# A three-layer transformer on one core: where softmax and query norms are divided out, and when weights are prepared

## What is computed

```
x = x + 0.5 * ffn(layernorm(x))          # two layers of local attention
x = x + attention(layernorm(x))          # 16 heads of 8, causal, softmax over 256 keys
x = x + 0.5 * ffn(layernorm(x))          # the same two layers

layer:     q, k, v = split(shift(x) @ wqkv)              # 8 heads of 64
           q, k = l2norm(q) * qs, l2norm(k) * ks         # per token and head
           q, k = rotary(q, k)
           x = x + local_attention(8 * q, k, v) @ wo     # windows of 64, look back one window
           x = x + (a * gelu(g)) @ w2 + b2               # a, g = layernorm(shift(x)) @ w1 + b1
attention: softmax(q k' / sqrt(8) + causal) @ v @ Wo + bo
```

## Time and profile before

| | before |
|---|---|
| median of 3 runs | 1858.02 us |
| lowest, highest | 1854.99, 1860.14 us |
| the profiled execution | 1866.13 us |
| its span, first to last instruction | 1864.3 us |
| mean granted clock of TensorE, of its full speed | 0.972 |

### The profile page before, as it was taken

The page is one execution under the profiler, slowest core; times in us unless marked ns, Lnnn a source line. Parts: engine busy times, 40 slices in busy tenths (PEclk is TensorE's granted clock), DMA queues, the critical chain, the costliest instruction groups (busy, mean ns, idle before and its releaser), DMA issues.

```text
span 1864.3 us, 51559 instructions
## 1 busy us (share of the span) xinstructions
PE 1680.3 (90%) x18560; PEld 1367.5 (73%) x18560; DVE 1479.3 (79%) x2938; ACT 1564.8 (84%) x4956; POOL 1286.7 (69%) x1528
## 2 busy tenths in 40 slices
PE   2798899989999999998988899899999999989987
PEld 2577778778877777777777677777687777777776
DVE  5788888688788687888889788876778775788886
ACT  1588799888999898998788888799999887988886
POOL 4899974487394657759998999920559570589991
PEclk9799999999999999999999999999999997999999
DMA  4101000000010000010100011000000000001000
GB/s 113 35 10 24 13 10 11 10 18 19 2 27 11 10 20 14 19 31 18 38 25 24 19 24 28 10 2 2 18 11 19 10 18 1 19 19 28 20 16 15
DMA packets 31701, 36.48 MB, mean 20 GB/s; under 512 B 7986, under 2 KB 18652, under 8 KB 31452
## 3 DMA queue, kind: packets, MB, share of 16 engines
q1 hardware_dynamic: 31452, 33.19, 7.4%
HBM read 5.91 MB, written 2.10 MB: 4 GB/s over the span
## 4 chain that ended last, share of the span: by engine, by line
POOL 37%; PE 23%; DVE 15%; ACT 15%; issue 9%; SPq 1%; DMA 0%; POOLq 0%; ACTq 0%; DVEq 0%
POOL rnorm L1031 13%; POOL parts L1021 11%; POOL parts L1035 8%; ACT probs L1090 8%; PE bank L1427 6%; PE bank L1510 4%; DVE parts L1358 4%; PE bank L1586 3%; POOL sums_floor L1028 3%; ACT turned L1108 2%; POOL rstd L1009 2%; DVE neg_max L1264 2%; PE bank L1546 2%; DVE sums L1365 2%; PE bank L1627 1%
## 5 line engine op out<-in xcount | busy, mean ns | idle before, releaser
L1090 ACT ACTIVATE probs<-bank,neg_max 128x128 f32<-128x128 f32 (+1 forms) x1536 | 584.7, 446 | 36.5 <-DVE neg_max L1264 35.5
L1021 POOL TENSOR_TENSOR parts<-parts 128x256 f32<-128x256 f32 x512 | 377.4, 763 | 161.8 <-DVE parts L1358 160.9
L1031 POOL TENSOR_TENSOR rnorm<-sums_floor,neg_half 128x8 f32<-128x8 f32 x256 | 431.9, 1687 | 21.3
L1090 ACT ACTIVATION_READ_ACCUMULATOR probs<-bank,neg_max 128x1 f32 x1536 | 401.5, 268 | 0.0
L1358 DVE TENSOR_TENSOR parts<-bank,rope 128x1024 f32<-128x1024 f32 x256 | 308.8, 1215 | 51.0 <-ACT squares L1137 49.7
L1264 DVE TENSOR_REDUCE neg_max<-bank 128x4 f32<-128x512 f32 (+1 forms) x448 | 287.5, 681 | 73.5 <-PE bank L1479 39.8
L1035 POOL TENSOR_TENSOR parts<-parts,rnorm 128x512 f32<-128x512 f32 x256 | 278.7, 1089 | 37.6 <-POOL rnorm L1031 1.3
L1510 PE MATMUL bank<-ident,probs 128*128 128x128 f32 x1792 | 253.5, 283 | 39.9 <-DVE probs L1279 19.4
L1108 ACT ACTIVATE turned<-bank 128x512 f32<-128x512 f32 x448 | 258.3, 661 | 34.1 <-PE bank L1510 33.5
L1510 PEld LDWEIGHTS bank<-ident,probs 128*128 128x128 f32 x1792 | 205.4, 145 | 78.3 <-issue 33.3
L1007 POOL TENSOR_SCALAR var_eps<-mean_var 128x2 f32<-128x2 f32 x112 | 32.3, 289 | 318.6 <-DVE mean_var L1297 313.6
(11 more groups left out here) (119 smaller groups left out, 3873.4 us busy)
## 6 DMA issues: line engine op xcount, KB each, us to landing
between<-val SPq DMA_DIRECT2D x192, 128.0 KB, 2.3
x_sb<-in_L_attn_x_dram SPq DMA_DIRECT2D x16, 128.0 KB, 2.7
out_dram<-x_sb SPq DMA_DIRECT2D x16, 128.0 KB, 1.9
raw_qkv<-in_L_ffn_wqkv_dram SPq DMA_DIRECT2D x2, 768.0 KB, 5.5
raw_w<-in_L_ffn_w_dram SPq DMA_DIRECT2D x2, 341.0 KB, 4.3
wo<-in_L_ffn_wo_dram SPq DMA_DIRECT2D x2, 256.0 KB
rope<-in_rope_dram SPq DMA_DIRECT2D x1, 256.0 KB, 3.0
w<-in_L_ffn_w_dram SPq DMA_DIRECT2D x2, 128.0 KB
```

The lines of the kernel that those rows point to most:

```text
L1021: last = nc.gpsimd.tensor_tensor(joined[:, :, dst], joined[:, :, dst], sines[:, :, src], ALU.add)
L1031: nc.gpsimd.tensor_tensor(rnorm[:, u], sums_floor[:, u], neg_half[:], ALU.pow).then_inc(sems["pool_step"], 1)
L1090: last = nc.scalar.activation(probs[:, u, block:block + wide].rearrange("p b j -> p (b j)"), bank[:, at:at + P * wide], ACT.Exp, bias=neg_ ...
```

## The change

- **Queries.** `rope_scale` of a q step ends with the power, which goes to a new buffer `q_norm`; the product over 512 columns stays for k only. `row_max` in local attention multiplies the 128x4 maxima by those inverse norms, and `exp_scores` takes them as a per-row scale.
- **Full attention.** The values get a ninth column of ones (`valf`), so that the product gives the row sum too. The turned probabilities (128x128) are now the stationary operand and nine columns of values move: 12 products a unit. The accumulators of the exponentials, the 64 reciprocals on their sums, the spreading products and ACT's copy of them go. DVE takes the reciprocal of the ninth columns in PSUM and scales 128x64 elements. The result has tokens in rows, so a new step **OT** turns it, two blocks a sequence, with a copy on ACT; WOF is one product in place of four; VALF moves 128 weight columns in place of 512, and its copy is as narrow.
- **Preparing.** The third, padded set of `wf` becomes an unpadded `wv`. `COME` holds times for READY 15 and 18, which it did not, and for LNX. The transfers of `bv` and `Wo` come ahead of the bias pieces, of which there are 24 in place of 32 transfers.
- **The order.** `passes` has new durations, and `START_AT`, `STRETCH`, `DUE`, `PHASE_DUE` and `LATER` (now 176 entries) new numbers, so all four orders differ.

```diff
 COME = {
-("READY", 12, 0): 19.0, ("READY", 21, 0): 37.0, ("FOLD", 2, 0): 37.0, ...
+("LNX", 0, 0): 8.5, ("READY", 12, 0): 19.5, ("READY", 15, 0): 19.5, ("READY", 18, 0): 19.5, ("READY", 20, 0): 35.0,
+("FOLD", 2, 0): 35.0, ...
 def passes(step):
     if kind == "X":
-        return [(DVE, 0.61), (ACTE, 0.92 if is_full(ph) and n % 3 else 1.4)]
+        return [(DVE, 0.61 if is_full(ph) else 0.83), (ACTE, (0.74 if n % 3 else 1.06) if is_full(ph) else 1.4)]
     if kind == "V":
-        return [(PE, 1.08), (ACTE, 0.28), (DVE, 0.34)] if is_full(ph) else [(PE, 0.97), (ACTE, 0.5)]
+        return [(PE, 1.5), (DVE, 0.4)] if is_full(ph) else [(PE, 0.97), (ACTE, 0.5)]
-LATER = {}
+LATER = {(0, 0): 75.49, (0, 1): -11.95, ...
 # rope_scale, POOL
+                if step[3] % 2 == 0:
+                    pool.wait_ge(sems["pool_step"], count("pool_step", step))
+                    if left_by(step) is not None:
+                        pool.wait_ge(sems["bank_filled"], count("bank_filled", left_by(step)))
+                    nc.gpsimd.tensor_tensor(q_norm[set_of(step)][:, step[3] // 2], sums_floor[:, u], neg_half[:],
+                                            ALU.pow).then_inc(sems["rope_ready"], 1)
+                    return
 # exp_scores, ACT
-                    last = nc.scalar.activation(probs[...], bank[:, at:at + P * wide], ACT.Exp, bias=neg_max[:, u, row:row + 1],
-                                                accum_out=prob_sum[:, u, row:row + 1])
+                    if is_full(ph):
+                        last = nc.scalar.activation(dst, bank[:, at:at + P * wide], ACT.Exp, bias=neg_max[:, u, row:row + 1])
+                    else:
+                        t, h = row % 2, UNIT * (k // 2) + row // 2
+                        last = nc.scalar.activation(dst, bank[:, at:at + P * wide], ACT.Exp, bias=neg_max[:, u, row:row + 1],
+                                                    scale=q_norm[set_of(step)][:, t, h:h + 1],
+                                                    accum_out=prob_sum[:, u, row:row + 1])
 # row_max, DVE, local attention
+                nc.vector.tensor_reduce(dst, src, AX, ALU.max, negate=True).then_inc(sems["vector_step"], 1)
+                dve.wait_ge(sems["vector_step"], count("vector_step", step))
+                nc.vector.tensor_tensor(dst, dst, norms, ALU.mult).then_inc(sems["max_ready"], 1)
 # values, PE, full attention
-                    for t in range(TILES):
-                        for h in range(UNIT):
-                            nc.tensor.matmul(bank[at:at + PAD_D, T + P * t:T + P * (t + 1)],
-                                             prob_inv[:, i, row:row + 1].to_broadcast([P, PAD_D]), ident[:], ...
-                    for t in range(TILES):
-                        for h in range(UNIT):
-                            last = nc.tensor.matmul(bank[at:at + PAD_D, P * t:T], val[a][:, t, PAD_D * (UNIT * m + h):...],
-                                                    turned[:, u, of:of + T - P * t], ...
+                    for h in range(UNIT):
+                        for n, (t, keys) in enumerate(((0, 0), (1, 0), (1, 1))):
+                            at, of = (FULL_D + 1) * (UNIT * t + h), P * (3 * h + n)
+                            last = nc.tensor.matmul(bank[:, at:at + FULL_D + 1], turned[:, u, of:of + P],
+                                                    valf[a][:, keys, UNIT * m + h], start=(keys == 0), stop=(keys == t),
+                                                    skip_group_check=True)
 # scale_heads, DVE
-                nc.vector.tensor_tensor(o_full[set_of(step)][:, m], bank[:, 0:T], inverse[:], ALU.mult)
+                nc.vector.reciprocal(inv, heads[:, :, :, FULL_D:FULL_D + 1]).then_inc(sems["vector_step"], 1)
+                dve.wait_ge(sems["vector_step"], count("vector_step", step))
+                nc.vector.tensor_tensor(o_full[...][:, :, cols]..., heads[:, :, :, 0:FULL_D], inv.to_broadcast(...), ALU.mult)
 # dense, PE
-                    for c in range(CHUNKS):
-                        last = nc.tensor.matmul(bank[:, 0:T], w[:, c], o[:, c], start=(c == 0), stop=(c == CHUNKS - 1))
+                if kind == "OT":
+                    for t in range(TILES):
+                        last = nc.tensor.transpose(bank[:, P * t:P * (t + 1)], o_full[set_of(step)][:, t], ident[:])
+                if kind == "WOF":
+                    last = nc.tensor.matmul(bank[:, 0:T], wof[:], y_t[s], start=True, stop=True)
-                    last = split_matmul(bank[:], hi[:, tok], lo[:, tok], wf_hi[:, 2], wf_lo[:, 2], True)
+                    last = split_matmul(bank[:, 0:C], hi[:, tok], lo[:, tok], wv_hi[:, 0], wv_lo[:, 0], True)
```

More of the change, by code:

```diff
@@ L109, in dense_parts @@
     return front, back
-DENSE = {"FOLD", "WO", "LNH", "LNT", "W1", "W2", "WOF", "XADD", "STATE", "Q", "VAL", "R", "QF", "VALF"}
+DENSE = {"FOLD", "OT", "WO", "LNH", "LNT", "W1", "W2", "WOF", "XADD", "STATE", "Q", "VAL", "R", "QF", "VALF"}
 POOLED = DENSE | {"T", "V"}
@@ L165 @@
+COME = {("LNX", 0, 0): 8.5, ("READY", 0, 0): 10.0, ("READY", 2, 0): 9.0, ("READY", 6, 0): 19.5, ("READY", 12, 0): 19.5, ("READY", 15, 0): 19.5, ("READY", 18, 0): 19.5,
+        ("READY", 20, 0): 35.0, ("FOLD", 0, 0): 14.0, ("FOLD", 1, 0): 14.0, ("FOLD", 2, 0): 35.0, ("FOLD", 0, 1): 23.0}
 BEGIN = (1.5, 2.0, 1.0, 5.3)
@@ L286, in weights_of @@
         return [("FOLD", 0, 0, DENSE_LAYER[PHASES[ph][1]])]
-    if kind in ("QF", "VALF") and part == 0:
-        m = n // 2 if kind == "QF" else 2
-        return made(("wf_hi", m), ("wf_lo", m))
+    if kind == "QF" and part == 0:
+        return made(("wf_hi", n // 2), ("wf_lo", n // 2))
+    if kind == "VALF" and part == 0:
+        return made(("wv_hi", 0), ("wv_lo", 0))
     if kind == "QF" and part == 1:
-        return made(("biases", 0))
+        return made(("biases", 0), ("table", LAYERS - 1))
     if kind == "WOF":
@@ L361, in needs @@
                     wait(x, 1, x, 0)
-                    wait(unit, 0, x)
+                    if not is_full(ph):
+                        wait(unit, 0, x)
                 for x in turned_for(unit):
@@ L466, in takes @@
             if before is not None:
-                for z in [(y, 1) for y in exps_of(before)] if part == 0 else [(y, 0) for y in turned_for(before)] + [(before, 0)]:
+                for z in [(y, 1) for y in exps_of(before)] if part == 0 else [(y, 0) for y in turned_for(before)]:
                     if z not in done:
@@ L683, in emits @@
         "W2": [{}, {"state_ready": 1}],
+        "OT": [{}, {"heads_turned": 1}],
         "WOF": [{}, {"state_ready": 1}],
```

232 lines of the change are left out of this document (116 added, 116 removed), and 44 rows, old and new, of tables (DUE, LATER).

## The result

The changed kernel takes **2080.22 us** (median of 4 runs, 2072.03 to 2081.93) against 1857.83 (4 runs, 1854.99 to 1860.14): a ratio of 1.119, 95% interval 1.116 to 1.122. It is slower by 222 us, where 24 were forecast. The direction was right; the time lies far outside the range (1813 to 1922).

The account below looks back on a forecast made before the run. PE was taken to bound the kernel, except where queries and keys are made, which POOL paces. The span of 1864.3 + 68 (PE) - 29 (POOL) - 15 (start), converted, gave 1882 us; range 1813 to 1922.

Parts of the forecast that it names:

- I take 0.11: Full attention on PE: each of V's 24 full-load records takes 0.11 us, as PE runs near full clock; +91 us.
- slow rival: Orders stall on wrong durations, or the clock falls under thin products: 1913 us; stalling cases (1900 to 1945) had 0.20.
- bound of +229 us for V alone: Full attention on PE: upper bound if all V records stood 0.2 us apart, 4.8 us a unit.
- three signs of being wrong: 128-column loads closer than 0.11 us, PE's share passing 95%, or the start keeping its 30 us.
- The loads of V: Full attention on PE: 24 full loads make V 2.64 us a unit, +91 us of busy time, covered by nothing.
- ACT's second operand: Local attention: a per-row scale on 1024 exponentials, 0 to +102 us on ACT, upper end taken, not a bound.
- DVE's product: Local attention: 256 products on the maxima, each behind a wait, at most +61 us on DVE.
- POOL's relief: Queries and keys: 128 products fewer, -139 us of POOL's busy time, worth -29 us, the middle of -39 and -19.
- The queries' part: Query normalisation moved from POOL into local attention: -29 us from POOL, with no span added for ACT or DVE.
- The start: First sequence: the scheduler can put weight padding behind its normalisation, so PE begins earlier; -15 us (bounds 0 and -18).
- The order: New orders of all four engines: nothing added, called the widest unknown, with its ends left to rivals.
- The relief of ACT in full attention: 512 accumulator reads (48 us) and 64 copies (23 us) go from ACT; none counted, beside a longer PE.

Follow-up runs that it names:

- b_ones: The kernel before with earlier start and full-attention row sums made on PE by columns of ones, without exponential accumulators or ACT's copy: 1907.72 us, ratio 1.022.

## Why the prediction was wrong, step by step

**Where it failed: "PE runs near full clock in both kinds of stretch", so "I take 0.11".** The clock was read from the kernel before and kept for a kernel whose products had changed. The two prices of a thin record stood there (0.11 and 0.2) as if the clock came from outside and a V merely met it. The runs show that the V brings it about: the same 24 loads with 128 columns keep 0.978, with nine 0.907. It costs 130 us in the orders of before. In the changed kernel the low level lasts 422 - 104 = 318 us longer, by the same 0.44 an estimated 140 us, near the 137 that PE's busy time has over the sum. Of the 318, 54 columns in place of nine take back 196, and 93 to 98 us with them. The other 122 aren't parted: orders alone added 74 and 91 us of low level to the instructions of before. The slow rival named a falling clock in one sentence and let it end at 1913; it needed a price of its own. The bound of +229 us for V alone was in the text and did not enter the range. It read L1580's row as one "at the low level of the clock", which no row shows: the profile has 1.00 from 14.00 to 16.60 us, where those twelve records run. That V does take 0.21 a record at the low level (4.98 / 24) bears the number out, not the reading. None of the three signs of being wrong was about the clock, and none of them came.

**The loads of V: right on PE, too dear at the end.** A V at full clock lasts 2.59 us (2.64 forecast). The forecast for V alone was +91 us of PE's busy time, 96 of span at PE's share of 94.7%; the +68 of the sum is net of the narrower WOF and VALF. With 128 moving columns PE's busy time grew by 78 us and the end came 66 later. So "nothing covers it" is not quite so: PE's idle time gave back some 12 us.

**ACT's second operand: size right, place wrong.** It was taken at 0.1 us each (measured 0.09) and then counted at none, since ACT is "not a bound" at 86%. Alone it cost 53 us in the orders of before. DVE's product was counted only as a brake on POOL's gain, and cost 27. A share of the span says how much an engine works, not whether its work lies in a chain: maximum, exponential, reciprocal, turn and V follow on each other, and every engine's fixed order hands a delay on.

**POOL's relief: mis-sized.** -29 forecast, the middle of -39 and -19; -48 measured alone. Even the end of it without a cap by DVE was too small.

**The queries' part in all:** forecast -29; measured +48 in the orders of before, +30 where either kernel has orders searched for it, and -30 in the changed kernel's own orders. The forecast was a gain only because ACT and DVE stood at nothing in it.

**The start: right in mechanism, somewhat large.** -15 forecast, -9 measured, with the first turn before 17 us as said.

**The order: counted at 0.** It isn't small. The due times of before would have cost the changed kernel some 63 us more; those of the change cost the kernel before some 127. But that orders on wrong durations stall is not where most of the loss came from: with V at its full-clock length the kernel takes as long.

**The relief of ACT in full attention: none counted, and not measured.** ACT waits 76 us more for turned probabilities than before, which fits. But no run takes the accumulators away and changes nothing else: b_ones loads DVE at the same time.

Adding up what was measured in the orders of before: +66 (loads) + 130 (clock) + 48 (queries) - 9 (start) = 235 us, against 222. That this comes so near is partly luck. The changed kernel runs other orders, in which the queries' part measured -30 and not +48, and the narrower WOF and VALF, ACT's relief and what the new orders cost by themselves were never parted.

The Trainium skill, page "TensorE: Matmul & The Clock Gate", section "HAM oscillation — how this bites in real kernels", tells of a clock that falls when PE stands idle waiting for transfers. This trace differs: PE is 94.8 to 98.5% busy in the stretches at 0.71 to 0.80. What is thin here is what a busy PE streams, not its share of the time.

## What to carry to other kernels

A product with a full stationary operand and a few moving columns cost twice here: its loads, and the clock of all that runs around it, though it took only about a quarter of a busy PE's time. Price such a product at the low level of the clock too, and give that case a chance of its own; moving more columns than are needed brought most of the clock back. And an instruction on an engine that isn't the bound is free only if it isn't in a chain between engines that run in fixed orders: here 0.09 us on each of 1024 exponentials, on an engine at 84%, cost more than half of itself at the end. Orders made for one program are no fair test of another: one edit cost 48 us in some orders and gained 30 to 36 in others.

## What the runs showed of the hardware that was not expected

- More work made a kernel faster: 128 moving columns in place of nine, with all else the same, took 130 us off (2059.90 to 1930.31), with a granted clock of 0.978 in place of 0.907.
- PE's clock stood at its lower level with the engine 98% busy (0.74 in 350 to 450 us of that kernel).
- DVE's reciprocal costs by the column far more than other operations: 0.20 us for 8 columns, 1.75 for 256, so 6.3 ns a column. The page "VectorE: DVE Perf Modes" of the Trainium skill, section "First, the fixed hardware budget", says that a reciprocal repeats its dividing steps eight times; here it costs four times what a product of the same size does (1.75 against 0.43 us), which agrees with it in kind.
